# A conditioned two-layer sequence block in float32: one input pair loaded ahead of the first weight, two pairs of statistics products merged, and new orders on the engines

## What is computed

```python
h = noise_encoding(t, 128)                     # sin and cos of 5000*t*freqs, t has 16 values
h = silu(h @ W1 + b1) @ W2 + b2                # 128 -> 512 -> 512
scale, shift = h @ Wsc + bsc, h @ Wsh + bsh    # 512 -> 256 each, one row per sequence
o = silu(scale * layer_norm(x) + shift)        # layer_norm over both axes (256 x 256) of a sequence
o = o @ W_in + b_in
o = silu(scale * layer_norm(o) + shift)
return o @ W_out + b_out + x                   # x: 16 sequences of 256 x 256, float32
```

## Time and profile before

| | us |
|---|---|
| median of 3 runs (lowest, highest) | 81.68 (81.18, 85.28) |
| time of the profiled execution | 81.69 |
| span of the profiled execution | 79.9 |
| PE busy in the span | 73.7 |
| DVE, ACT, POOL busy | 63.3, 56.5, 44.1 |

### The profile page before, as it was taken

One profiled execution on the slowest core, in us unless ns is written; L12 is line 12 of the kernel. 1 busy time (PEld: TensorE's weight loads), 2 busy tenths in 40 slices (PEclk: granted clock), 3 DMA queues, 4 the chain that ended last, 5 costly groups with the idle time before them and its releaser, 6 DMA issues.

```text
span 79.9 us, 1304 instructions
## 1 busy us (share of the span) xinstructions
PE 73.7 (92%) x282; PEld 36.8 (46%) x282; DVE 63.3 (79%) x187; ACT 56.5 (71%) x177; POOL 44.1 (55%) x54
## 2 busy tenths in 40 slices
PE   4999899696999999999999999999999999999930
PEld 1367657384553445445453434435334444564400
DVE  1096299969999999999999992899995799870670
ACT  4211323699799899999998999996999995640000
POOL 6000079985859999999998989999103012000000
PEclk9999999999999999999999999999999999999999
DMA  1799999999700000302100700015006000365064
GB/s 10 268 433 404 427 388 400 414 398 410 281 12 4 0 0 0 131 0 86 45 0 4 271 8 0 0 64 199 0 0 263 0 0 0 131 251 208 28 253 178
DMA packets 4903, 11.92 MB, mean 149 GB/s; under 512 B 672, under 2 KB 928, under 8 KB 4768
## 3 DMA queue, kind: packets, MB, share of 16 engines
q1 hardware_dynamic: 4752, 11.33, 36.8%
q10 hardware_dynamic: 144, 0.52, 1.7%
HBM read 7.65 MB, written 4.19 MB: 148 GB/s over the span
## 4 chain that ended last, share of the span: by engine, by line
PE 72%; DMA 15%; SPq 6%; DVE 2%; issue 2%
PE acc L1066 33%; PE acc L1042 31%; DMA x_sb<-x_dram 15%; PE stat L1018 3%; PE acc L1077 2%; PE acc L1054 1%; DVE o_sb L777 1%; SPq L298 1%; SPq L296 1%; SPq L297 1%; SPq L300 1%; SPq L301 1%; SPq L299 1%; SPq L295 1%; SPq L293 1%
## 5 line engine op out<-in xcount | busy, mean ns | idle before, releaser
L461 ACT ACTIVATE act<-act,cond 128x256 f32<-128x256 f32 x64 | 35.8, 597 | 3.6 <-DVE act L772 2.0
L1066 PE MATMUL acc<-act,wout_sb 128*128 128x512 f32 x60 | 27.9, 600 | 0.0
L1042 PE MATMUL acc<-act,win_sb 128*128 128x512 f32 x56 | 26.9, 606 | 0.0
L332 POOL TENSOR_TENSOR rstd<-variance,minus_half 128x2 f32<-128x2 f32 (+1 forms) x14 | 10.4, 748 | 19.1 <-DVE variance L760 9.6
L347 POOL TENSOR_TENSOR act<-act,gamma_sb 128x512 f32<-128x512 f32 x13 | 16.4, 1274 | 1.3 <-issue 0.2
L1066 PEld LDWEIGHTS acc<-act,wout_sb 128*128 128x128 f32 x60 | 10.8, 190 | 12.2 <-issue 8.1
L485 ACT ACTIVATE squares<-acc,shift 128x256 bf16<-128x256 f32 x32 | 14.7, 465 | 0.6 <-DVE shift L754 0.5
L777 DVE SCALAR_TENSOR_TENSOR o_sb<-acc,const_sb,x_sb 128x512 f32<-128x512 f32 (+1 forms) x17 | 11.9, 714 | 3.6 <-PE acc L1066 3.0
L765 DVE SCALAR_TENSOR_TENSOR act<-acc,shift,gamma_sb 128x256 f32<-128x256 f32 x32 | 14.2, 474 | 0.6 <-ACT squares L485 0.6
L1042 PEld LDWEIGHTS acc<-act,win_sb 128*128 128x128 f32 x56 | 9.9, 190 | 10.0 <-issue 7.2
L772 DVE SCALAR_TENSOR_TENSOR act<-act,rstd,beta_ps 128x512 f32<-128x512 f32 x16 | 11.4, 742 | 2.8 <-issue 1.9
(11 more groups left out here) (65 smaller groups left out, 53.6 us busy)
## 6 DMA issues: line engine op xcount, KB each, us to landing
out_dram<-o_sb SPq DMA_DIRECT2D x15, 256.0 KB, 2.0
x_sb<-x_dram SPq DMA_DIRECT2D x7, 512.0 KB, 12.6
w_sb<-w_dram SPq DMA_DIRECT2D x1, 1024.0 KB, 6.2
wss_sb<-wss_dram SPq DMA_DIRECT2D x1, 768.0 KB, 8.4
x_sb<-x_dram ACTq DMA_DIRECT2D x1, 512.0 KB, 3.9
w_sb<-w_dram SPq DMA_DIRECT2D x1, 256.0 KB, 4.2
gamma_sb<-gamma_dram SPq DMA_DIRECT2D x1, 256.0 KB, 6.4
wss_sb<-wss_dram SPq DMA_DIRECT2D x1, 256.0 KB, 8.6
```

Source lines behind the costliest of these rows:

```text
L332: nc.gpsimd.tensor_tensor(rstd[:, i, 0:k], variance[:, i, 0:k], minus_half[:, 0:k], ALU.pow).then_inc(rstd_ready, 1)
L461: return nc.scalar.activation(buf[:, c, b], buf[:, c, b], ACT.Silu, bias=cond[:, 1, c, i:i + 1], scale=cond[:, 0, c, i:i + 1], **kw)
L1042: mm = nc.tensor.matmul(y_slot(p, c)[:].rearrange("p b s -> p (b s)"), win_sb[:, k, c * P:(c + 1) * P], act1[:, p, k].rearrange("p b s -> ...
L1066: mm = nc.tensor.matmul(bank_of(("O", p, c, 0, BP))[:].rearrange("p b s -> p (b s)"), wout_sb[:, k, c * P:(c + 1) * P], act2[:, p, k].rear ...
```

## The change

The number of arithmetic operations on DVE, ACT and POOL stays, and so do the layer products on PE. What is changed:

- SP: the load of x of pair 2 stands ahead of that of w_in.
- PE: `warm(3)`, `warm(3)` and `warm(6)` between the conditioning products are gone (12 of 24 products of zeros); `warm(8)` at the head and `warm(4)` ahead of the first layer stay.
- `STATS` has 17 entries in place of 19: "mean1" of group 3 goes with "mean2" of pair 0, and "mean1" of group 5 with "vars" of pair 2 and "mean2" of pair 3. With the merging the matrix for "mean1" of groups 3 and 5 is the other constant, and `deviation` of these groups multiplies by a factor (L659 in place of L658).
- ACT, DVE, POOL, PE: the same calls in another order, and other banks for the products (of pair 0's first layer banks 1 and 2 in place of 3 and 0).

The diff, cut to its core:

```diff
...
 SUMMED_BY_ACT = ()
 STATS = ((('mean1', 0),), (('var1', 0),), (('mean1', 1),), (('var1', 1),), (('mean1', 2),), (('var1', 2),), (('mean2',
-    0),), (('mean1', 3),), (('mean2', 1),), (('vars', 0), ('var1', 3)), (('mean1', 4),), (('vars', 1), ('mean2', 2),
-    ('var1', 4)), (('vars', 2), ('mean2', 3)), (('mean1', 5),), (('vars', 3), ('var1', 5), ('mean2', 4)), (('vars',
-    4), ('mean2', 5)), (('vars', 5), ('mean2', 6)), (('vars', 6), ('mean2', 7)), (('vars', 7),))
+    0), ('mean1', 3)), (('mean2', 1),), (('vars', 0), ('var1', 3)), (('mean1', 4),), (('vars', 1), ('mean2', 2),
+    ('var1', 4)), (('vars', 2), ('mean2', 3), ('mean1', 5)), (('vars', 3), ('var1', 5), ('mean2', 4)), (('vars', 4),
+    ('mean2', 5)), (('vars', 5), ('mean2', 6)), (('vars', 6), ('mean2', 7)), (('vars', 7),))
...
@@ -297,8 +297,8 @@
             sp.dma_start(wss_sb[:, 0:KH - 1], wss[:, 0:KH - 1]).then_inc(wss_in, 16)
             sp.dma_start(wss_sb[:, KH - 1:], wss[:, KH - 1:]).then_inc(wss_last_in, 16)
             sp.dma_start(beta_sb[:], beta).then_inc(beta_in, 16)
+            sp.dma_start(x_sb[:, 2], x[2]).then_inc(x_in[2, 0], 16)
             sp.dma_start(win_sb[:], w_in).then_inc(win_in, 16)
-            sp.dma_start(x_sb[:, 2], x[2]).then_inc(x_in[2, 0], 16)
             sp.dma_start(x_sb[:, 3], x[3]).then_inc(x_in[3, 0], 16)
             sp.dma_start(x_sb[:, 4], x[4]).then_inc(x_in[4, 0], 16)
             sp.dma_start(wout_sb[:], w_out).then_inc(wout_in, 16)
...
@@ -491,15 +491,15 @@
 
             encode()
             hidden_silu()
+            copy_gamma()
             copy_h2_rows()
-            copy_gamma()
             copy_cond_rows()
             copy_beta()
             activate1(0, 0, 0)
             activate1(0, 0, 1)
+            activate1(0, 1, 0)
+            sum_w_in(0)
             activate1(0, 1, 1)
-            sum_w_in(0)
-            activate1(0, 1, 0)
             sum_w_in(1)
             activate1(1, 0, 0)
             activate1(1, 0, 1)
...
-            aggregate1(1, 0)
-            add_b2()
             weigh_gamma(0, 0, 1, 1)
+            weigh_gamma(0, 0, 0, 1)
+            deviation(1)
             negate_mean(1)
-            deviation(1)
             spread1(1, 1)
             spread1(1, 0)
             weigh_gamma(1, 0, 0, 2)
-            weigh_gamma(0, 0, 0, 1)
-            stats1_variance(1)
+            weigh_beta(0, 0, 1, 1)
             weigh_beta(0, 0, 0, 1)
             add_b_cond()
-            weigh_beta(0, 0, 1, 1)
+            stats1_variance(1)
+            bn_stats1(2, 0)
             bn_stats1(2, 1)
-            bn_stats1(2, 0)
+            weigh_beta(1, 0, 0, 2)
             aggregate1(2, 1)
-            weigh_beta(1, 0, 0, 2)
             aggregate1(2, 0)
             bn_stats1(3, 0)
+            bn_stats1(3, 1)
+            deviation(2)
+            negate_mean(2)
+            aggregate1(3, 0)
+            spread1(2, 1)
             weigh_rowsum0(0)
-            deviation(2)
-            aggregate1(3, 0)
-            negate_mean(2)
             spread1(2, 0)
-            spread1(2, 1)
-            bn_stats1(3, 1)
             weigh_rowsum1(0)
-            stats1_variance(2)
             aggregate1(3, 1)
             weigh_gamma(2, 0, 0, 2)
+            stats1_variance(2)
+            bn_stats1(4, 1)
             mean_shift2(0)
-            bn_stats1(4, 1)
+            deviation(3)
+            bn_stats1(5, 1)
             weigh_rowsum0(1)
-            deviation(3)
+            spread1(3, 1)
+            aggregate1(5, 1)
+            weigh_rowsum1(1)
...
         @block.tensor
@@ -1118,14 +1118,11 @@
             pe.wait_ge(zeros_set, 1)
             warm(8)
             mean_of_b_in()
-            warm(3)
             hidden1()
-            warm(3)
             stats(0)
             hidden2_rows()
             stats(1)
             hidden2()
-            warm(6)
             stats(2)
             cond_rows_begin()
             cond_rows_end()
@@ -1135,87 +1132,85 @@
             layer1_half(0, 1, 0, 0)
             layer1_half(0, 0, 0, 0)
             layer1_half(0, 1, 0, 1)
+            layer1_half(0, 1, 1, 0)
+            stats(4)
             layer1_half(0, 0, 0, 1)
-            stats(4)
             layer1_half(0, 0, 1, 0)
-            layer1_half(0, 1, 1, 0)
+            layer1_half(0, 0, 1, 1)
             stats(5)
-            layer1_half(0, 0, 1, 1)
+            layer1_half(0, 1, 1, 1)
             stats(6)
-            layer1_half(0, 1, 1, 1)
+            layer1(1, 0, 0)
+            layer1(1, 0, 1)
             stats(7)
-            layer1(1, 0, 0)
             stats(8)
-            layer1(1, 0, 1)
-            stats(9)
             layer1(1, 1, 0)
             layer1(1, 1, 1)
+            layer1(2, 0, 0)
             layer1(2, 1, 0)
-            layer1(2, 0, 0)
+            stats(9)
+            layer1(2, 1, 1)
             layer1(2, 0, 1)
-            layer1(2, 1, 1)
             stats(10)
+            layer2(0, 1, 0)
...
```

More of the change, by code:

```diff
@@ L381, in _ @@
             weigh_gamma(4, 0)
+            centre1(5, 1)
             weigh_gamma(4, 1)
+            weigh_gamma(5, 1)
             weigh_gamma(5, 0)
             power(7)
-            centre1(5, 1)
-            weigh_gamma(5, 1)
             weigh_beta(5, 1)
@@ L782, in _ @@
             bn_stats1(0, 1)
+            aggregate1(0, 0)
+            aggregate1(0, 1)
             centre_b_in()
-            aggregate1(0, 1)
-            aggregate1(0, 0)
+            deviation(0)
             negate_mean(0)
-            deviation(0)
+            spread1(0, 1)
             spread1(0, 0)
-            spread1(0, 1)
             stats1_variance(0)
@@ L855, in _ @@
-            copy_deviation(4)
-            weight2(1, 1, 1)
-            square_deviation(4)
-            weight2(1, 0, 1)
-            spread1_pairs(4)
-            weight2(1, 0, 0)
-            bn_stats1(7, 1)
-            variance2(1)
-            stats1_variance(4)
+            stats1_variance(3)
+            add_beta(2, 1)
+            variance2(0)
+            weight2(0, 1, 0)
+            aggregate1(4, 1)
+            weight2(0, 1, 1)
+            bn_stats1(5, 0)
+            weight2(0, 0, 0)
@@ new lines, in _ @@
+            aggregate1(4, 0)
+            aggregate1(5, 0)
+            normalise2(0, 0)
+            weight2(0, 0, 1)
+            copy_deviation(4)
+            weigh_rowsum0(2)
+            deviation(4)
+            normalise2(0, 1)
+            negate_mean(4)
+            square_deviation(4)
+            weigh_rowsum1(2)
+            spread1_pairs(4)
+            weight2(1, 1, 0)
+            weight2(1, 0, 0)
+            weight2(1, 0, 1)
+            mean_shift2(2)
+            stats1_variance(4)
@@ L864, in _ @@
+            bn_stats1(6, 1)
+            bn_stats1(7, 0)
+            variance2(1)
+            bn_stats1(7, 1)
+            weight2(1, 1, 1)
+            aggregate1(7, 0)
+            bn_stats1(6, 0)
             finish(0, 0, 0, 2)
-            mean_shift2(2)
-            bn_stats1(7, 0)
+            aggregate1(6, 1)
+            weigh_rowsum0(3)
+            normalise2(1, 0)
+            weigh_rowsum1(3)
             normalise2(1, 1)
-            normalise2(1, 0)
-            bn_stats1(6, 0)
@@ L870, in _ @@
-            weigh_rowsum0(3)
-            weight2(2, 1, 0)
-            weigh_rowsum1(3)
-            aggregate1(7, 0)
-            weight2(2, 1, 1)
-            finish(0, 1, 0, 2)
-            mean_shift2(3)
-            aggregate1(6, 0)
-            add_beta(4, 0)
-            variance2(2)
-            add_beta(4, 1)
-            bn_stats1(6, 1)
-            aggregate1(7, 1)
-            weight2(3, 1, 1)
-            aggregate1(6, 1)
-            weight2(3, 1, 0)
-            add_beta(5, 0)
-            weight2(2, 0, 0)
+            aggregate1(6, 0)
@@ L888, in _ @@
+            aggregate1(7, 1)
+            finish(0, 1, 0, 2)
+            add_beta(4, 0)
+            mean_shift2(3)
+            weight2(2, 1, 1)
+            weight2(2, 1, 0)
+            add_beta(4, 1)
             deviation(5)
             weight2(2, 0, 1)
-            negate_mean(5)
-            weigh_rowsum0(4)
-            normalise2(2, 1)
-            copy_deviation(5)
-            weigh_rowsum1(4)
-            square_deviation(5)
-            spread1_pairs(5)
-            finish(1, 1, 0, 2)
@@ L898, in _ @@
-            mean_shift2(4)
-            stats1_variance(5)
-            finish(1, 0, 0, 2)
-            normalise2(2, 0)
-            weight2(3, 0, 1)
+            finish(1, 0, 0, 2)
+            copy_deviation(5)
+            weight2(2, 0, 0)
+            square_deviation(5)
+            variance2(2)
+            add_beta(5, 0)
+            weigh_rowsum0(4)
+            negate_mean(5)
+            finish(1, 1, 0, 2)
+            spread1_pairs(5)
+            weigh_rowsum1(4)
+            weight2(3, 1, 1)
@@ L903, in _ @@
+            weight2(3, 0, 1)
+            weight2(3, 0, 0)
+            mean_shift2(4)
+            variance2(3)
+            stats1_variance(5)
```

(23 more changed lines are left out.)

284 lines of the change are left out of this document (132 added, 152 removed), and 12 rows, old and new, of the table PRODUCTS.

## The result

| | before | changed |
|---|---|---|
| median of six executions | 81.74 us (81.18 to 85.28) | 84.03 us (82.74 to 84.18) |
| ratio | 1 | 1.0239, 95% interval 1.0184 to 1.0294 |
| profiled execution, span | 81.69, 79.9 | 84.16, 82.4 |

The forecast was 81.5; the change costs about 2 us. Every ratio in this document leaves out executions over 1.5% above the fastest of their own kernel (three of the changed kernel's six, nine of twelve in e9_five_only), so where a kernel has executions of two kinds, its median and its range tell more than its ratio.

What follows compares the result with a forecast made beforehand. PE was taken as the bound from 21 us, after a wait on x of pair 3. Terms 0 + 0 + 0.25 - 0.22 - 0.24 = -0.21 took 81.69 to 81.5 us; 8-in-10 range 80.0 to 83.9.

Steps and rivals of the forecast that it cites:

- The zeros: Between conditioning products: removing 12 zeros products, which stand where PE waits, was worth 0 at the first activation, -0.3 to +0.4.
- Rival 1: PE's clock: without the zeros PE runs at half rate through conditioning and perhaps the halves; +1.9, 83.4 us, chance 0.25.
- far end: Half rate lasting through the seven half products, 0.86 us each instead of 0.43, puts stats(5) at 22.7, +2.9.
- The swap: Loads on SP: x of pair 2 ahead of w_in lets DVE begin earlier, but the gain becomes idling; worth 0.
- DVE after x of pair 3: DVE's list from x of pair 3's landing at 17.66: squares fed later, PE idles at stats(8); +0.25, -0.4 to +0.8.
- idle PE of about 0.6: Sign of the DVE term: PE idle about 0.6 us ahead of the eight column product near 23.4.
- Two products fewer: Merged statistics on PE: -0.22 for the one at 40.05, -0.24 for an earlier group 5 mean; bounds -0.46 to +0.6.
- Rival 2: Load of x of pair 3 lands earlier, DVE starts about 16.4 rather than 17.66; 80.5 us, chance 0.15.
- Rival 3: DVE's full lists do not fit: merged stats(11) waits (+0.6), start takes +0.2; 82.3 us, chance 0.10.

Runs made afterwards that it cites:

- e9_five_only: Changed kernel with one block of five zeros products ahead of the first hidden product and no other put back; 82.2 us, ratio to before 0.9966.
- e2: Kernel before with the same 12 products of zeros removed, nothing else; 84.04 us, ratio to before 1.0275.
- e3: Changed kernel with only the six zeros products behind the second hidden product put back; 81.76 us, ratio to before 0.9970.
- e12: e8 without the three zeros products behind the first hidden product; 81.72 us, ratio to before 0.9975.
- e4: Changed kernel with only the two threes of zeros around the first hidden product put back; 81.43 us, ratio to before 0.9945.
- e1: Changed kernel with all 12 products of zeros put back (3, 3 and 6); 81.69 us, ratio to before 0.9973.
- e5: e1 with the load of w_in ahead of x of pair 2 again; 81.69 us, ratio to before 0.9983.
- e6: e1 with the merge of pair 0's second mean and group 3's mean undone; 82.71 us, too scattered for a ratio.
- e7: e1 with DVE's list reordered near the old order so that stats(5) is fed first; 81.91 us, ratio to before 1.0006.
- e8: e1 with five zeros products instead of three ahead of the first hidden product; 80.98 us, ratio to before 0.9897.

## Why the prediction was wrong

- **The zeros, 0 (-0.3 to +0.4).** This is the step that failed. "They stand where PE waits anyway" is true of their own time and beside the point: e2 takes them out of the old kernel and loses as much as the whole change (median 84.04 against 81.61). Without them the granted clock falls to half in the waits where they stood. Rival 1 named the mechanism, with a chance of 0.25 and a price of +1.9; the chance was too low. I took the absence of a fall in the rows as evidence of a kind, but with the zeros in place those rows could not show one.
- **Rival 1's numbers.** Its far end, "stats(5) at 22.7", was measured as 22.74, and that is in part luck. The first half product starts at 17.54, not at about 16.4, 1.1 us later than rival 1 had it; and the rate comes back for the last three of the seven halves, which take 1.66 us where half rate would take about 2.7 (an estimate, three quarters of the 3.62 for four), 1.1 us less. The two misses cancel. Its time, 83.4, was 0.6 short of the measured 84.03. The lateness of cond was under-sized: ACT starts 1.72 us late (16.40 against 14.68), not 0.9, and e3 against e12 makes 1.4 us at the end of 2.03 us there.
- **When the rate falls and rises.** The Trainium skill, TensorE: Matmul & The Clock Gate, What's actually happening, says that the default is throttled and activity releases it. The prediction had the trace agreeing at the start only. The changed kernel, e2, e4 and e9 agree for the fall as well: each shows the half rate in or right behind the waits where zeros stood. The profiled execution of e1 is harder to fit: PE works there without a wait until 17 us and stays at half rate as long, while in e5, with waits in the same stretch, the rate is up at the first row product (1.08 us). How busy PE is does not tell by itself, in these traces, when the rate rises.
- **The swap, 0.** Right: e5 against e1. In e6 (swap kept) bn_stats1 of pair 2 begins at 14.40, and DVE then idles 1.27 us for x of pair 3, in e5 (swap undone) 15.01 and 0.66. The gain became idling, as forecast.
- **DVE after x of pair 3, +0.25 (-0.4 to +0.8).** Under-sized, at the edge of its bounds. In e5, which has x of pair 3 at 17.77, stats(5) goes at 20.17 (forecast 19.75), the first square at 21.69 (21.35), and the product behind stats(8) at 24.09, where the same timeline of before has it at 23.32: +0.77. (The prediction compared with 23.47 from the chain, which starts a product where the one ahead of it ends; there e5 has 24.25, forecast 23.7.) The form was right, the idle PE of about 0.6 is the 0.55 in the row. What I left out is 0.3 us of issue ahead of weigh_rowsum0. But the remedy that the term suggests falls with e7.
- **Two products fewer, -0.22 and -0.24.** Right in kind, under-sized. The product behind pair 4's third takes 0.29 with no wait (0.36 before), and the 16 column product at 36.91 has none either. From the product behind stats(8) to the end e5 gains 0.77 - 0.05 = 0.72 on before, forecast 0.46: 0.47 up to the product at 43.14 and 0.25 behind it. Here two misses cancel in part as well: the total of e5, 81.72, stands near the forecast of 81.5 because DVE's term was 0.5 too small and this one 0.3.
- **Rival 2** (x of pair 3 by 16.5) came true as a condition, at 16.2, and gave nothing that can be seen, because PE at half rate was later still. In e8 it landed early too (10.6 us) with the rate up: 81.00 us in the profiled execution, and 80.86 in e12, where rival 2 said 80.5.
- **Rival 3** did not happen: no wait at either full list. DVE's 6.8 us for it were added up without rows, so only the outcome can be compared.

## What to carry to other kernels

Filler products need not be idle work that fills a wait: before removing any, ask what PE's rate is in the products behind them, and compare the same product's time at both rates (here 1.08 and 1.93) instead of looking for a fall that the fillers prevent. The dearest place for a low rate need not be where it falls: here the first dense stretch behind cost 2.0 us and the lateness up to it 1.4, of which a late load can hide a part. Moving one feeder ahead in a full list pays only if the next feeder is not already the bound.

## What was unexpected

- The column of granted clock can read 1.00 over a stretch at half rate: e1 at 9.66, row product 1.93 us against 1.08. Spacing of a known product is the safer reading.
- x of pair 3 takes one of two times from issue to landing in kernels with equal loads: 11.8 to 12.0 us (before, e4, e5, e6, e7) or 10.4 to 10.8 (changed, e1, e2, e3, e8 to e12). It is not tied to the swap: e1 and e6 have the same loads in the same order, and 10.5 and 11.9. The rule that rival 2 took from the Trainium skill, DMA: Bandwidth & Descriptors, Queues, rings and completion order, that a transfer's parts on the engines finish independently, would fit; no run here tells the cause.
- Open as well: why executions of one kernel differ in when the rate first rises (e1 is late in 5 of 12, if all five are as the profiled one).
